# Maxima moved by DMA in the first layer, and a 256-column rounded first gram block in the second

## What is computed

```python
# layer 0: 77 text rows and 435 image rows of the context, each with its own softmax
q = heads(x @ Wq.T); k = heads(text @ Wk.T); k_ip = heads(ip @ Wk_ip.T)    # v, v_ip likewise
out = softmax(q @ k.T * D**-.5) @ v + softmax(q @ k_ip.T * D**-.5) @ v_ip
x = out @ Wo.T + bo + x
# layer 1: 508 text rows, 4 image rows
p = softmax(q @ k_t.T * D**-.5)
text_out = p @ v_t
qsem = l2norm(p @ text)                              # per head, 512 wide
sem = qsem @ l2norm(ip).T
p_ip = softmax(q @ k_ip.T * D**-.5 + 0.5 * sem) * mask
y = (text_out + p_ip @ v_ip) @ W_out + b_out + x
```

## Time and profile before

| | |
|---|---|
| median of 3 runs | 1715.8 us (1711.35 to 1715.96) |
| the profiled execution, its own time | 1714.97 us |
| its span, first to last instruction | 1713.2 us |
| granted TensorE clock, mean | 0.989 of full speed |
| busy: PE, DVE, ACT, POOL | 1586.2, 1277.6, 1113.8, 441.6 us |
| chain that ended last | PE 77%, ACT 16%, issue 2% of the span |

### The profile page before, as it was taken

The page is one execution under the profiler, slowest core; times in us unless marked ns, Lnnn a source line. Parts: engine busy times, 40 slices in busy tenths (PEclk is TensorE's granted clock), DMA queues, the critical chain, the costliest instruction groups (busy, mean ns, idle before and its releaser), DMA issues.

```text
span 1713.2 us, 26860 instructions
## 1 busy us (share of the span) xinstructions
PE 1586.2 (93%) x8608; PEld 1211.7 (71%) x8608; DVE 1277.6 (75%) x3548; ACT 1113.8 (65%) x2323; POOL 441.6 (26%) x1233
## 2 busy tenths in 40 slices
PE   6888999999988899999998889999998889999993
PEld 3554489999455459999755537999965544899991
DVE  2797378887789538888779835888877982788875
ACT  1797367775399547777459926777727972677760
POOL 0343023322044112233114402333203430232320
PEclk9999999999999999999999999999999999999996
DMA  9010310010411230001221032000031103000100
GB/s 311 24 37 15 111 58 21 20 35 1 123 39 37 59 95 25 20 20 30 54 83 37 29 91 69 20 21 22 22 111 39 37 15 111 14 22 22 34 2 16
DMA packets 47780, 83.62 MB, mean 49 GB/s; under 512 B 4868, under 2 KB 12308, under 8 KB 47640
## 3 DMA queue, kind: packets, MB, share of 16 engines
q1 hardware_dynamic: 44968, 76.77, 14.6%
q10 hardware_dynamic: 2672, 5.13, 0.9%
HBM read 41.49 MB, written 34.10 MB: 44 GB/s over the span
## 4 chain that ended last, share of the span: by engine, by line
PE 77%; ACT 16%; issue 2%; DVE 1%; DMA 1%; SPq 1%; POOL 0%; DVEq 0%; ACTq 0%
PE ps_w L938 46%; PE ps_s L938 12%; PE ps_t L938 11%; PE ps_b L938 7%; ACT probsT_high L522 5%; ACT probsT L530 5%; ACT probs L541 3%; ACT q_slots L515 3%; PE ps_m L938 1%; DMA q_slots<-out_all 1%; DMA q_slots<-probsT_low 1%; SPq L350 0%; ACT probs L618 0%; POOL probsT_low L433 0%; SPq L312 0%
## 5 line engine op out<-in xcount | busy, mean ns | idle before, releaser
L714 DVE TENSOR_TENSOR probsT_low<-probsT,probsT_high 128x512 fp32r<-128x512 f32 x560 | 397.5, 710 | 80.4 <-ACT probsT L530 76.3
L522 ACT ACTIVATE probsT_high<-ps_t 128x512 fp32r<-128x512 f32 x640 | 382.3, 597 | 114.1 <-PE ps_t L938 112.1
L938 PE MATMUL ps_w<-gram,probsT_high 128*128 128x416 f32 (+2 forms) x1280 | 388.1, 314 | 0.0
L530 ACT ACTIVATE probsT<-ps_t 128x512 f32<-128x512 f32 x640 | 384.1, 600 | 0.0
L938 PE MATMUL ps_w<-gram_low,probsT_high 128*128 128x384 f32 (+2 forms) x1280 | 352.0, 303 | 0.0
L453 POOL TENSOR_SCALAR exp_bias<-row_max 128x1 f32<-128x1 f32 x320 | 123.4, 385 | 695.9 <-DVE row_max L772 695.9
L558 ACT ACTIVATE probs<-ps_s,exp_bias 128x508 f32<-128x508 f32 x320 | 218.9, 685 | 123.5 <-POOL exp_bias L453 85.9
L938 PE MATMUL ps_t<-q_slots,k_slots 98*128 98x512 f32 x640 | 256.3, 421 | 0.9 <-ACT probsT L530 0.5
L938 PEld LDWEIGHTS ps_w<-gram_low,probsT_high 128*128 128x128 f32 (+1 forms) x1280 | 243.0, 190 | 10.9
L938 PEld LDWEIGHTS ps_w<-gram,probsT_high 128*128 128x128 f32 (+1 forms) x1280 | 241.0, 188 | 9.1
L938 PE MATMUL ps_w<-gram,probsT_low 128*128 128x400 f32 (+2 forms) x1280 | 245.4, 314 | 0.0
(11 more groups left out here) (166 smaller groups left out, 2011.6 us busy)
## 6 DMA issues: line engine op xcount, KB each, us to landing
q_slots<-parts_q SPq DMA_DIRECT2D x128, 96.0 KB
k_slots<-parts_k SPq DMA_DIRECT2D x128, 96.0 KB
parts_k<-probsT_high SPq DMA_DIRECT2D x16, 512.0 KB, 4.4
parts_k<-probsT_high SPq DMA_DIRECT2D x24, 256.0 KB, 4.3
parts_q<-probsT_low SPq DMA_DIRECT2D x8, 512.0 KB, 3.8
parts_q<-x_sb SPq DMA_DIRECT2D x8, 512.0 KB, 4.6
k_slots<-probsT_high SPq DMA_DIRECT2D x24, 128.0 KB, 3.9
parts_q<-probsT_low SPq DMA_DIRECT2D x12, 256.0 KB, 4.2
```

Of the source, the lines that this page charges most:

```text
L522: nc.scalar.activation(probsT_high[1 - par][:, t, :], ps_t[:, t % 2, :], ACT.Exp, scale=SCALE)
L530: nc.scalar.activation(probsT[:, t, :], ps_t[:, t % 2, :], ACT.Exp, scale=SCALE).then_inc(pt_block[l], 1)
L714: nc.vector.tensor_tensor(probsT_low[1 - par][:, t, :], probsT[:, t, :], probsT_high[1 - par][:, t, :].bitcast(F32), ALU.subtract).then_in ...
L938: return nc.tensor.matmul(out, lhsT, rhs, start=start, stop=stop)
```

## The change

First layer. The transpose of the maxima on PE and ACT's copy are gone. DVE writes the maxima of a head as two planes of 128x4 (`row_max0`), and SP moves each with a DMA straight to its row of the query slot (`shift` on SP), 128 pieces of 16 bytes per row. The row's column is then 4 times the partition plus the chunk, so that the queries of a chunk are every fourth column of the slot; `scores_chunk` takes them at that step. PE waits for the rows before the first transposed block, DVE before it writes the maxima anew. The scores run half a head further ahead: in step n PE computes half 1 of head n+2 and half 0 of head n+3. Queries and keys stand in one tile and in one scratch tensor, and a slot is loaded by one DMA for both. The stores of the batch's result move behind the slot loads of the next batch's first layer.

Second layer. The first gram block is kept doubled and rounded, with its rest beside it, 256 columns in one fp32r product with `probsT_high` alone, in two pairs of chunks: one at the head of a step, one before gram product 2. DVE weighs both 128-column parts with the probabilities less half of their rounded value. ACT makes that half (`half_rounded`) and POOL subtracts it in place (`less_half_high`). Orders on all engines are written anew: the transpose of the maxima comes behind gram product 0, scores stand ahead of the transposed blocks, and DVE's last product read stands before the last low part.

```diff
-SLOT_LOADS = 2 * 16
+SLOT_LOADS = 16
+SHIFTS = SHIFT_ROWS * 16
...
-        q_slots, k_slots = sb("q_slots", [ALL_ROWS, SLOTS, S], F32R), sb("k_slots", [ALL_ROWS, SLOTS, T], F32R)
+        slots = sb("slots", [ALL_ROWS, SLOTS, 2, S], F32R)
+        q_slots, k_slots = slots[:, :, 0, :], slots[:, :, 1, :]
...
+        def rows_loaded(eng, b, k, turn):
+            eng.wait_ge(rows_in[k % SLOTS], SHIFTS * (TURNS * b + turn + k // SLOTS + 1))
...
# SP
-                for slot, src in ((q_slot[k], scratch[f"q{l}"]), (k_slot[k], scratch[f"k{l}"])):
-                    sp.dma_start(slot[0:SCORE_ROWS, :].bitcast(F32), src[:, turn, :, k, :])\
-                        .then_inc(slots_in[l][k], 16)
+                sp.dma_start(slots[0:SCORE_ROWS, k, :, :].bitcast(F32),
+                             scratch_of[l][:, turn, :, k, :, :].rearrange("p d i s -> d p i s")).then_inc(slots_in[l][k], 16)
...
-                if l == 0 and b is not FIRST:
-                    store_outputs(b)
+                if l == 0:
+                    shift(batch, 0, 0)
+                    shift(batch, 1, 1)
...
                         load_slots(batch, l, turn + 1, k)
+                        if l == 0:
+                            shift(batch, SLOTS * turn + k + 2, (k + 2) % SLOTS)
...
+                if l == 0 and b is not FIRST:
+                    store_outputs(b)
+
+            def shift(b, n, k):
+                sp.wait_ge(max_half, 2 * (HEADS * b + n + 1) + CREDIT)
+                for r in range(SHIFT_ROWS):
+                    sp.dma_start(q_slots[SHIFT_ROW + r:SHIFT_ROW + r + 1, k, :].bitcast(F32),
+                                 row_max[0][k % 2][:, r, :].bitcast(F32)).then_inc(rows_in[k], 16)
...
# POOL, second layer, after the bias of chunk 0
+                def less_half_high(of, head):
+                    pool.wait_ge(half_high_in, head + 1)
+                    nc.gpsimd.tensor_tensor(probs[of][:, :, 0:P], probs[of][:, :, 0:P], half_high[:, :, :].bitcast(F32),
+                                            ALU.subtract).then_inc(less_half, 1)
...
# ACT, second layer, ahead of shift
+                def half_rounded(of, head):
+                    act.wait_ge(p_chunk, SC * (head + 1) + CREDIT)
+                    act.wait_ge(less_half, head)
+                    nc.scalar.activation(half_high[:, :, :], probs[of][:, :, 0:P], ACT.Copy, scale=0.5).then_inc(half_high_in, 1)
...
# DVE, first layer
-                if scores and (use or transposed or last is FIRST):
-                    maxima0(b, n + 2, 0, par)
+                if scores:
+                    maxima0(b, n + 2, 1, par)
...
                     lowT(b, 0, n, par, 0)
-                if scores:
-                    maxima0(b, n + 2, 1, par)
+                if scores_next and not first:
+                    rows_loaded(dve, b, k + 1, turn)
+                    maxima0(b, n + 3, 0, 1 - par)
...
# DVE, second layer
+                def first_block_used(pair):
+                    dve.wait_ge(b_done, 2 * g + pair + 1)
+                    for i in range(2):
+                        c = 2 * pair + i
+                        last = nc.vector.tensor_tensor_reduce(out=weighed[i],
+                                                              in0=ps_b[:, 2 * P * i:2 * P * i + 2 * P].rearrange("p (a k) -> p a k", a=2),
+                                                              in1=probs[par][:, c, 0:P].unsqueeze(1).to_broadcast([P, 2, P]),
...
                 for c in range(SC):
+                    if use and c == 2:
+                        first_block_used(1)
                     if use and c < 3:
                         products_used(c)
+                    if c == 3 and transposed:
+                        lowT(b, 1, n, par, 1)
                     if scores:
                         maxima(c)
...
+                    if c == 1 and transposed:
+                        lowT(b, 1, n, par, 0)
+                if transposed:
+                    lowT(b, 1, n, par, 2)
+                if use:
+                    products_used(3)
+                if transposed:
+                    lowT(b, 1, n, par, 3)
...
# PE, first layer
-                if scores:
-                    scores_half(0)
...
+                if scores:
+                    scores_half(2, 1)
...
                 if transposed:
+                    rows_loaded(pe, b, k + 1, turn)
                     scoresT_of(0, g, k, 0)
...
-                if scores:
-                    scores_half(1)
+                if scores_next and not first:
+                    scores_half(3, 0)
...
-                if scores:
-                    pe.wait_ge(max_half, 2 * (g + 3) + CREDIT)
-                    head_maxT(0, par)
...
# PE, second layer
-                    for c in range(SC):
-                        last = mm(ps_b[:, P * c:P * c + P], probsT[:, 0, P * c:P * c + P], gram00[:, :], True, True)
+                def first_block(pair):
+                    pe.wait_ge(zb_done, 2 * g + pair + CREDIT)
+                    for i in range(2):
+                        c = 2 * pair + i
+                        last = mm(ps_b[:, 2 * P * i:2 * P * i + 2 * P], probsT_high[par][:, 0, P * c:P * c + P],
+                                  gram00[:, :, :].rearrange("p a k -> p (a k)"), True, True)
```

More of the change, by code:

```diff
@@ L106, in sem @@
             return ctx.enter_context(nc.semaphore(name))
-        scratch = {n: nc.dram_tensor(f"parts_{n}", [3, TURNS, D, SLOTS, S], F32, kind="Internal").ap()
-                   for n in ("k0", "q0", "k1", "q1")}
+        scratch_of = [nc.dram_tensor(f"parts{l}", [3, TURNS, D, SLOTS, 2, S], F32, kind="Internal").ap() for l in range(2)]
+        scratch = {f"{n}{l}": scratch_of[l][:, :, :, :, i, :] for l in range(2) for i, n in enumerate("qk")}
         vip_dram = nc.dram_tensor("vip_rows", [IPN, C], F32, kind="Internal").ap()
@@ L149, in build @@
         dump = sb("dump", [P, 16])
+        ip_shift = probsT[0:1, 0, :]
         heads_out = probsT[:, :, 0:C]
@@ L155, in build @@
         stat = sb("stat", [P, nd, 8])
+        weighed = [stat[:, 32 * i:32 * i + 32, :].rearrange("p n e -> p (n e)").rearrange("p (a k) -> p a k", a=2) for i in range(2)]
         root = sb("root", [P, nd + IPN])
@@ L410, in _, with step0 @@
                                     pattern=[[-1, P]], channel_multiplier=1).then_inc(built, 1)
-            def step0(b, n, k, turn, use, transposed, scores, last=FIRST):
+            def step0(b, n, k, turn, use, transposed, scores, scores_next, last=FIRST):
                 par = k % 2
@@ L454, in step1 @@
                             .then_inc(bias_in, 1)
+                        if c == 0 and transposed:
+                            less_half_high(1 - par, g + 1)
+                if transposed and not scores:
+                    less_half_high(1 - par, g + 1)
                 if use:
@@ L568, in step1 @@
                 for c in range(SC):
+                    if scores and c == 0:
+                        exps(0)
+                    if first and c == 1:
+                        gram_rows(b, 0)
+                    if second and c == 0:
+                        gram_rows(b, 3)
+                        v1_rows(b, 0)
                     if transposed:
                         expT(b, 1, n, par, c)
-                    if scores and c < 2:
-                        exps(c)
-                    if second and c == 0:
-                        gram_rows(b, 3)
-                    if second and c < TB - 1:
+                    if second and c in (1, 2):
                         v1_rows(b, c)
-                if first:
-                    gram_rows(b, 0)
+                    if scores and c == 1:
+                        exps(1)
                 if scores:
```

142 lines of the change are left out of this document (77 added, 65 removed).

## The result

The changed kernel takes 1677.8 us (median of 4 runs, 1675.4 to 1679.1), the kernel before beside it on the same chip 1715.4 (4 runs): a ratio of 0.978, 95% interval 0.976 to 0.980. That is 37.6 us less; 52 were forecast. The profiled run took 1678.2 us, with a span of 1676.4.

A forecast was written before the change was run, and what follows sets the result against it. Bounds were taken as a loop through DVE and PE in the first layer, PE in the second. Savings of 32 + 23 - 3 = 52 us from 1715.0 give 1663, forecast 1664 us; range 1650 to 1680, 8 in 10 1640 to 1700.

The forecast's parts named there:

- I take nothing: First-layer score products: weight loads at every fourth column were costed at nothing, at most one more load time of 0.19 us.
- The 4.82 of DVE's work: First layer: sum of DVE's work per head in us, by starts, from which a period of 5.0 was taken.
- Rival A: First layer: each strided weight load takes twice its 0.19 us, all showing; period 5.35, total 1689 us; chance 0.12.
- DVE without waits over 0.3: First layer: sign expected if the forecast held, no DVE wait over 0.3 us, beside a period of 4.9 to 5.1.
- weight loads of the scores over 0.2 us: Score products on PE: a sign that would show the forecast wrong.
- Slack was forecast as 3.5 us against 2.5: First layer: rows of maxima have 3.5 us until their product; issue 0.67 plus landing 1.8 make 2.5, 1.0 to spare.
- Rival D: First layer: rows land late and PE waits; at 5.1 us the step is 5.9, total 1727 us; chance 0.12.
- 7.3 + 2.75 us: Second layer: DVE's loop from the second gram product's end, 7.3, then PE to the next one, 2.75; together 10.05.
- the bound passes from PE to DVE: Second layer: DVE's loop of 10.05 us sets the period above PE's floor of 9.92; 0.27 of 0.40 is left.
- keep 0.40: Second layer: the last three heads of a batch have no scores and keep the whole PE saving of 0.40 us each.
- the 0.40 of the signs: Second layer: the forecast is wrong if DVE's first-block reduction takes over 0.40 us; 0.34 was forecast.
- the missing transpose of the maxima and the scores that are already there give most back: Refill: the first transposed score product comes about 1.6 us later, mostly regained; 0.8 us per batch, +3 us in all.

The follow-up runs named there:

- the two doses: Two runs adding second-layer work to the changed kernel: one more DVE reduction of 128 columns per first-block pair (1700.4 us), or each first-block PE product done twice (1701.8 us).

## Why the prediction was right, and where it was off

The direction and the range (1640 to 1700) held; the time came out 14 us above the 1664, near the upper end of the narrower 1650 to 1680. That the sum came so near is in part luck: the first layer and the fills fell 8.5 and 10.8 us short, and the second layer and the stretch between the layers, for which no gain was forecast, gave 2.4 and 3.5 back.

- **First layer, 32 us forecast, 23.5 measured.** The step that failed is "I take nothing", the term for weight loads at a column step. They take 0.32 us instead of 0.19, the two pairs lengthen, and DVE gets its scores later: 0.12 us a head. With neighbouring columns the period is 4.99, beside the forecast's 5.0, but that agreement is partly luck. The 4.82 of DVE's work counted a low part at 0.83 that takes 0.60 to 0.69 now: before, POOL's own low part ran beside it until 479.06, and now that one is over (499.33) before DVE's begins (499.53). DVE's work is 4.57 to 4.74, and what neighbours in a loop lose is 0.25 to 0.42 where 0.18 was allowed. Rival A had the mechanism with the wrong size: each load is 0.125 dearer, not 0.19, and of the 0.27 us a head that show on PE, 0.12 reach the period, so it is 5.11 and not 5.35. The rule of the Trainium skill ("SBUF — State Buffer", section on the DMA port swizzle) pointed the right way; the runs do not show that its 16-byte lines are the cause. "DVE without waits over 0.3" held (0.27), and the sign of being wrong, weight loads of the scores over 0.2 us, was there.
- **Rows in time.** Slack was forecast as 3.5 us against 2.5. In the changed kernel the medians are 3.82 against 2.53; in the head shown above the maxima end at 504.42, the rows land at 507.35, 0.4 later than in its neighbours, and the product comes at 508.24. The landing is 2.0 (forecast 1.8), and the margin 1.3 us, of which four issues in place of two take 1.06. Rival D's price was right in kind, and its chance rested on a landing of 4.4 that did not occur.
- **Second layer, 23 us forecast, 25.4 measured.** The period is 9.95 instead of 10.05. The loop was drawn as 7.3 + 2.75 us and is 7.03 + 2.93, so two errors partly cancel. That "the bound passes from PE to DVE" was only half of it: the two doses put both within 0.16 us of the period. That the last three heads "keep 0.40" was wrong: the last period went from 9.02 to 8.96 only; 18 others gained 0.35. The first-block reduction takes 0.34 by start (its written 0.42 is over the 0.40 of the signs, where the 0.34 forecast was by start), ACT's rounding 0.63 (0.585 was forecast) and POOL's subtraction 1.29, hidden, as forecast; the exponential of the second chunk (702.89 on ACT) shows no wait for its bias.
- **Fills, +3 us forecast, +13.8 measured.** This lies outside the term's bounds (-2 and +8), and the failed step is "the missing transpose of the maxima and the scores that are already there give most back". They gave nothing back: the refill without a stretch at the lower clock lost 2.3 us, where 1.6 were to be lost and half of that regained. All first scores of a fill pass through one pair of banks, `ps_s`, so each half waits for DVE's maxima of the half before: 1.70 us with nothing of PE's between. Behind two of the three waits the clock fell to 1.2 GHz for 3.4 us, 1.6 us more each. Moving that half behind work that was ready gave 8.6 us of the 10.2 us that the refills had lost. The first fill's +3.6 us stays open in part: its waits (1.47, 1.47, 0.62, 0.60) and the 10.2 us at the lower clock come with the first-layer part, but the two were not separated. With that part alone, though, the fill took 62.8 and had no stretch near 36 us; with the second-layer part alone it took 62.3, with 3.4 us at that clock from 36.1 and 6.8 from 53.2.
- The stretch between the layers and the end moved by -3.5 and +1.8 us; the forecast had no term for them. The end goes with the length of its stretch at the lower clock (34.1 us from 1634.3 after, 30.7 from 1672.5 before). In the twelve profiles, counted from the start of L845 (0.15 us more than in the table), it is 46.1 and 46.3 us with 23.9 at that clock, 47.6 to 47.9 with 27.3, 48.4 to 48.6 with 30.7 and 50.2 to 50.6 with 34.1. What sets that length was not tested. Of the -3.5 us between the layers, 1.7 are the granted clock: in the last batch the kernel before is at 1.2 GHz for 3.4 us from 1406.3, and its stretch takes 64.34 us where the other three take 62.62. The rest is 0.44 us a batch (62.62 to 62.18), which no run separates.

## What to carry to other kernels

Where a row is read by an engine that is nearly full, its new access pattern is part of the cost: look whether the load may start while a long product runs. Here the same 0.125 us cost nothing behind a running product of 512 columns, and all of itself behind small products or where the load was held by a wait. Running ahead pays in the steady part and has to be paid in the fill: list for the first steps what each half waits for, and put ready work of another kind between. To test which of two engines bounds a stage, add a known dose to each; here both showed most of it, so a gain on one of them alone would be small (0.08 to 0.16 us a head, an estimate from the doses).

## What was not expected of the hardware

- 128 fp32 weight columns at a step of four take 0.315 to 0.320 us to load, neighbouring ones 0.190; the transposed score products, whose loads did not change, stay at 0.191.
- A DMA of 2 KB between two tiles lands 2.0 us after its issue in 128 pieces of 16 bytes, 1.8 in 64 such pieces, and 2.0 in 128 pieces of 4 bytes. An issue holds SP for 0.6 us, and it was the number of issues that made the rows late.
- A wait of 1.47 us on PE was followed by 3.4 us at 1.2 GHz in two refills of three and not in the third, at the same place in the program. Over all kernels with this wait it was 16 refills of 24. In the five kernels that have refills of both kinds at an else equal length, those with the stretch took 1.5 to 1.7 us more.
